# Waits of the products with V moved ahead of the pair's feed-forward share

## What is computed

```python
xn = layernorm(x)
q, k, v = split(xn @ w_qkv)                    # 16 heads of 16
q, k = spectral_filter(q), spectral_filter(k)  # a fixed 16x16 matrix once the mask is known
attn = softmax(q @ k.T / 4)                    # per batch and head: 2048 x 2048
a = (attn @ v) @ w_out + b_out
h = relu(xn @ W_fc.T) ** 2                     # 1024 wide
y = h @ W_proj.T
# 5 steps of mem = 0.9 * mem + y - reset, spikes counted
out = x + a + counts / 5
```

## Time and profile before

| | us |
|---|---|
| median of three runs | 1831.87 |
| lowest, highest | 1831.08, 1835.48 |
| profiled execution, its time | 1832.95 |
| profiled execution, its span | 1831.2 |
| PE busy in the span | 1811.6 (99%) |
| DVE busy | 1420.3 (78%) |
| ACT busy | 1075.5 (59%) |
| POOL busy | 710.2 (39%) |

### The profile page before, as it was taken

How to read it: one execution, slowest core, us unless ns; L and a number is a source line. 1 busy time by engine, 2 the same in 40 slices (tenths; PEclk the granted TensorE clock), 3 DMA queues, 4 the chain that set the end, 5 groups by cost and what they waited for, 6 DMA issues and landing times.

```text
span 1831.2 us, 35316 instructions
## 1 busy us (share of the span) xinstructions
PE 1811.6 (99%) x14308; PEld 1092.2 (60%) x14308; DVE 1420.3 (78%) x1781; ACT 1075.5 (59%) x1182; POOL 710.2 (39%) x948
## 2 busy tenths in 40 slices
PE   8989999999999999999999999999999999999998
PEld 5655556665555566655555666555556665555666
DVE  6767877787778777877787778777877787788765
ACT  3426666666666666666666666666666666666662
POOL 1002344444333444443334444433344444333445
PEclk9989999999999999999999999999999999999999
DMA  5660222222112222221122222211222222112223
GB/s 176 226 206 17 45 44 43 45 41 43 32 22 45 44 43 45 39 44 28 26 45 44 43 45 39 44 27 27 44 45 43 45 39 44 25 30 44 44 87 105
DMA packets 86175, 98.82 MB, mean 54 GB/s; under 512 B 50870, under 2 KB 64950, under 8 KB 82042
## 3 DMA queue, kind: packets, MB, share of 16 engines
q1 hardware_dynamic: 82844, 93.42, 23.4%
q10 hardware_dynamic: 3168, 3.15, 0.5%
HBM read 70.80 MB, written 20.99 MB: 50 GB/s over the span
## 4 chain that ended last, share of the span: by engine, by line
PE 97%; DMA 1%; DVE 1%; issue 0%; SPq 0%; ACT 0%; ACTq 0%; DVEq 0%
PE ring L651 32%; PE banks L661 28%; PE ring L641 18%; PE banks L719 6%; PE banks L724 6%; PE banks L597 2%; PE ring L803 2%; PE ring L609 1%; PE ring L643 1%; PE ring L588 0%; DMA attnT<-x 0%; DMA qst<-shiftT 0%; PE ring L565 0%; DMA filt<-logits 0%; DVE attnT L846 0%
## 5 line engine op out<-in xcount | busy, mean ns | idle before, releaser
L881 DVE TENSOR_REDUCE pmax<-ring 128x2 f32<-128x1024 f32 x1000 | 1176.3, 1217 | 335.4 <-PE ring L643 332.4
L521 ACT ACTIVATE probs<-ring 128x1024 f32<-128x1024 f32 x1024 | 993.3, 1022 | 642.1 <-PE ring L651 639.1
L651 PE MATMUL ring<-qst,kst 66*128 66x512 f32 x2048 | 615.2, 422 | 5.1 <-DMA qst<-shiftT 5.1
L661 PE MATMUL banks<-probs,vst 128*32 128x256 f32 x8192 | 548.3, 385 | 0.1
L651 PEld LDWEIGHTS ring<-qst,kst 66*128 66x128 f32 x2048 | 345.5, 188 | 262.5 <-issue 215.2
L641 PE MATMUL ring<-kst,qst 64*128 64x512 f32 x1000 | 387.8, 467 | 0.0
L643 PE MATMUL ring<-kup,qup 64*128 64x512 f32 x1000 | 387.3, 467 | 0.0
L661 PEld LDWEIGHTS banks<-probs,vst 128*32 128x32 f32 x8192 | 213.8, 109 | 213.1 <-issue 124.5
L432 POOL TENSOR_TENSOR lif<-lif 128x256 f32<-128x256 f32 x32 | 21.6, 676 | 793.4 <-ACT y_sb L537 793.4
L641 PEld LDWEIGHTS ring<-kst,qst 64*128 64x128 f32 x1000 | 183.2, 184 | 159.1 <-DVE pmax L881 82.2
L643 PEld LDWEIGHTS ring<-kup,qup 64*128 64x128 f32 x1000 | 183.1, 183 | 0.0
(11 more groups left out here) (76 smaller groups left out, 683.0 us busy)
## 6 DMA issues: line engine op xcount, KB each, us to landing
qup<-qk_scratch SPq DMA_DIRECT2D x252, 64.0 KB, 4.1
qst<-qk_scratch SPq DMA_DIRECT2D x124, 128.0 KB, 4.1
kst<-qk_scratch SPq DMA_DIRECT2D x62, 256.0 KB, 5.9
qk_scratch<-attnT SPq DMA_DIRECT2D x32, 256.0 KB
kup<-qk_scratch SPq DMA_DIRECT2D x64, 128.0 KB, 6.4
qk_scratch<-probs SPq DMA_DIRECT2D x16, 256.0 KB
qst<-shiftT SPq DMA_DIRECT2D x256, 2.0 KB
attnT<-o_turned SPq DMA_DIRECT2D x256, 16.0 KB, 1.9
```

Source lines behind the costliest of these rows:

```text
L521: act.activation(probs[:, s % PS, :], score_slot(g), ACT.Exp, scale=SCALE).then_inc(exp_done, 1)
L651: mm = pe.matmul(score_slot(g)[:, c * BLK:(c + 1) * BLK], kst[b][:, kt * P:(kt + 1) * P], qst[b][:, q:q + BLK], start=True, stop=True)
L661: mm = pe.matmul(po[32 * j:32 * (j + 1), half * D:(half + 1) * D], vst[b][:, kt, :], quarters[:, j], start=(kt == 0), stop=(kt == TB - 1))
L881: dve.tensor_reduce(pmax[:, tile, first:first + 2], unit_slot(g).rearrange("p (c e) -> p c e", c=2), AX, ALU.max).then_inc(mx_taken, 1)
```

## The change

The waits that stood in `times_v` and ahead of it, between the maxima and the products with V, now stand between the scores and the feed-forward piece. The two waits on `exp_done` of a pair become one, for the later of its two steps. What is computed and the order of the products are the same.

```diff
@@ times_v @@
                 quarters = probs[:, s % PS, :].rearrange("p (t j q) -> p j t q", j=4, q=32)
-                pe.wait_ge(exp_done, g + 1 + 2)
                 for j in range(4):
@@ pair @@
                         scores(x, x % STEPS, sb_)
+                valued = [v for v in (s - LAG, s - LAG + 1) if v >= 0 and (v < STEPS or not last)]
+                for v in valued:
+                    if v % TB == 0:
+                        pe.wait_ge(po_taken, 2 * i + v // TB)
+                        pe.wait_ge(vst_ready, i + 1 + v // STEPS)
+                if valued:
+                    pe.wait_ge(exp_done, STEPS * i + valued[-1] + 1 + 2)
                 beside()
...
-                for v in (s - LAG, s - LAG + 1):
-                    if v >= 0 and (v < STEPS or not last):
-                        if v % TB == 0:
-                            pe.wait_ge(po_taken, 2 * i + v // TB)
-                            pe.wait_ge(vst_ready, i + 1 + v // STEPS)
-                        times_v(STEPS * i + v, v % STEPS, b if v < STEPS else 1 - b)
+                for v in valued:
+                    times_v(STEPS * i + v, v % STEPS, b if v < STEPS else 1 - b)
```

## The result

| | before | after |
|---|---|---|
| median, us | 1831.78 (4 runs) | 1872.13 (4 runs, 1869.37 to 1875.09) |
| profiled execution, span, us | 1831.2 | 1873.3 |

The ratio is 1.0216, with a 95% interval of 1.0203 to 1.0229: 40 us slower, where 38.4 were forecast (1870.3).

What follows compares the result with a forecast made beforehand. PE was taken to bound the kernel, with 0.05 us slack a pair. Stalls on `po_taken`, 31 x 0.63 + 31 x 0.61 = 38.4 us, other moved waits 0, on the median 1831.87 gave 1870.3 us, range 1859 to 1880.

Steps and rivals of the forecast that it cites:

- The bound: Heads: PE sets the end; its loop runs through the exponential of g, leaving 0.05 us slack a pair.
- The moved `exp_done` waits at 0: Products with V and feed-forward piece: these waits are already met, so removing or moving them costs 0.
- `vst_ready`: Ahead of the feed-forward piece: POOL's copy starts 45 us ahead of the pair, so moving this wait costs 0.
- `po_taken`, the term of the sum: Feed-forward piece at s = 18 and 34: waits for DVE's transpose; delay 0.66 and 0.68 us before the slack.
- What comes back: Second maxima: no longer held by the exponential of g, so 0.05 us of each delay returns.
- the lower bound: Stalled pairs: no 0.10 start-up and 0.13 given back instead of 0.05; 0.44 us each, 27 us, 1859.
- Count and keeping: Heads: 31 stalls at s = 18, 31 at s = 34; later pairs keep 3.27 us, so the delay stays.
- The sum: All heads: 31 x 0.63 + 31 x 0.61 = 38.4 us, giving 1870.3 us, 2.1% slower.
- V starting earlier: Products with V: without a wait on their first load, 0.13 us gained in 500 pairs, 65 us; 1805; 4%.
- A swallowed delay: Ahead of the second maxima: slack of 0.3 halves each stall, 20 us, 1852, 4%; nothing left, 1832, 2%.
- The clock: PE after each stall: granted clock falls for two pairs, 193 us, 2060; 3%.
- A dearer stall: Pairs after a stall: late reductions hold the scores, second stall in half the places; 58 us, 1889; 5%.

Runs made afterwards that it cites:

- the run with the longer take-out: Changed kernel with an extra maximum over the same 256 columns of po ahead of each take-out on DVE: 1891.25 us, ratio 1.0322.

## Why the prediction was right

- **The bound.** PE is the engine that sets the end, and its loop passes through the exponential of g. The shorter and the halved exponential show it.
- **The moved `exp_done` waits at 0.** Shown by the run that moves them alone. `vst_ready` was never moved alone ahead of the piece; with only `po_taken` there the time is the same as with both, so it adds nothing that the times can tell.
- **`po_taken`, the term of the sum.** Released load 0.05 behind the take-out: measured 888.36 - 888.31. Start of the product 0.10 behind an uncovered load: from the piece's load to the first maxima it takes 889.00 - 888.36 = 0.64, where from its first product it took 869.01 - 868.47 = 0.54, so 0.10. First maxima behind the start of the scores: 2.25 instead of 1.57, a delay of 0.68 as worked out.
- **What comes back.** On average the first maxima come 0.67 later and the pair is 0.62 longer, so 0.05 comes back, as in the sum. The size is right in part by luck, since the rows were read wrongly: the forecast said that the maxima's starts would stand 0.29 apart, and they stand 0.34 apart, as before. The gain lies behind the second maxima (889.67 - 889.34 = 0.33 instead of 0.36 in the pair shown, 0.32 instead of 0.37 on average), in the gap of which the lower bound would have given back 0.13.
- **Count and keeping.** 62 places, 0.61 us at each s = 18 and 0.63 at each s = 34, the two terms of the sum. The other pairs keep their length, so nothing was given back.
- **The sum.** 38.4 worked out, 38.5 in the stalled pairs, 39.4 in the profile's heads, 40 in the medians.
- **In the list of waits** I had expected 35 to 50 us in 62 entries; the loads show 52.1. That number counts idle time of loads which a running product covers.
- **The rivals.** V starting earlier: no, by the run with `exp_done` alone. A swallowed delay: no, beyond the 0.05; that rival's price was also off, since a slack of 0.3 leaves 0.67 - 0.30 = 0.37 us and not 0.33, 23 us and not 20. The clock: granted at 1.00 from 137 us on, with holes of 0.41 us between products, and still at 1.00 with holes of 0.7 us in the run with the longer take-out. A dearer stall: no, pairs apart from s = 18 and 34 keep their length.

The Trainium skill, "TensorE: Matmul & The Clock Gate", section "Step-by-step: what each phase is for", has PE pull weight loads ahead of running products when the row groups don't conflict or the load goes to the background buffer. The runs agree for the scores and for the feed-forward piece behind them, also where the load carries a wait that is met (868.24 for a product at 868.47 in the earlier trace rows). Ahead of V no load was pulled, with a wait (869.71 in the earlier trace rows) and without one (889.67 after). The prediction put this down to every change in the kind of product, which goes too far: the feed-forward piece is another kind than the scores, and its load is pulled. The waits are not what keeps V's loads back; what does, no run shows.

## What to carry to other kernels

A wait that is met costs nothing here. One that blocks costs the time from where the held product would have started to the releaser's end, here 869.00 - 868.47 = 0.53 us, plus 0.05 until the load is released and 0.10 for a start without cover, less the slack behind it. So ask of every hoisted wait where its releaser ends, and count what used to run in between. A wait can be moved freely as long as it stays behind that end: one piece later here is the difference between 40 us and 0. And a wait behind which the load always starts some 0.05 us after the releaser's end is a bound, however full the engine looks: starting the producer's first half earlier was worth 22 us.

## What the runs showed of the hardware

- A load on PE that has to wait is issued 0.05 us behind the end of the transpose on DVE that releases it (888.36 - 888.31), and 0.06 behind that of the exponential on ACT (869.29 - 869.23 in the earlier trace rows). With no cover the feed-forward product starts 0.10 us later than with a load that was issued under the product before, as read from the distance to the first maxima; no run takes this term apart.
- A maximum and a transpose of DVE with no wait between them overlap by some 0.08 us (892.71 + 0.41 against 893.04), so the instruction added costs 0.33 and not its 0.41 us.
- Two exponentials of 512 columns on ACT, with only a met wait between them, start 0.50 us apart at 0.60 each: the pair takes 1.09 us from the first start to the last end, against 1.02 for one of 1024. I had reckoned 1.19.
